# Causal attention in a decoder layer: every fourth head multiplies its weights by the values in fp32, the others in fp16 halves; one engine makes each low half, and ScalarE copies the keys

## The chip, the core and the metric

The kernel runs on one core of a Trainium2 chip. The core has five engines that run at the same time and wait for each other by semaphores: TensorE (PE in the rows; PEld is its weight load), VectorE (DVE), ScalarE (ACT), GpSimd (POOL) and SyncE (SP), which here starts the DMAs. The metric is the device time of one execution in microseconds (us).

## The reference

A decoder layer on x (4 x 512 x 512): attention, cross attention to a context, and a mixture of experts, each followed by a layer norm. Only the first part is touched by the change:

```python
q = (x @ Wq).reshape(B, S, 16, 32).transpose(0, 2, 1, 3)
c_kv = x @ Wkv_down
k = (c_kv @ Wk_up).reshape(B, S, 16, 32).transpose(0, 2, 1, 3)
v = (c_kv @ Wv_up).reshape(B, S, 16, 32).transpose(0, 2, 1, 3)
# 24 of the 32 columns of q and k are rotated (rope)
scores = jnp.where(causal, -jnp.inf, jnp.einsum('bhqd,bhkd->bhqk', qf, kf) * scale)
out = jnp.einsum('bhqk,bhkd->bhqd', softmax(scores), v)
```

## The kernel before

Fp32 numbers are multiplied on TensorE as two fp16 halves: a high half (the rounded number, a copy by ScalarE) and a low half (the number minus its high half, by VectorE or GpSimd). The attention runs over 4 batches of 512 tokens. In a batch there are 16 heads, each with 512 queries and keys in 4 blocks of 128. A loop body holds the heads of batch b and, woven between them, the projections of batch b+1; the first batch's projections stand ahead of the loop, and the last batch's heads behind it. What each engine does, and in which order, is written out by hand in the lists A_PE, A_ACT, A_DVE and A_POOL (L79 to L102), as steps "kind.number". An engine works its list strictly from left to right. Semaphores hold a step until what it needs is there.

The steps of one head i:

- `bq.i` (PE, L935): scores with queries on the partitions, into three PSUM banks; `max.i` (DVE, L1473): their row maxima, four reductions (nmf). The maxima of four heads are transposed (`mT`) and copied behind the queries (L1483), so that the second scores come out with the maximum taken off.
- `bk.i` (PE, L956): scores with keys on the partitions, 1280 columns for the causal triangle.
- `exp.i` (ACT, L1182): the exponential, PSUM to pf (fp32, 1280 columns, one of two buffers by i % 2).
- `hi.i` (ACT): phi, the fp16 copy of pf. `lo.i`: plo = pf - phi, columns 0 to 895 by POOL (L753) and 896 to 1279 by DVE (L1487). The next exp in the same buffer waits for both parts.
- `pv.i` (PE, L971): 10 pairs of blocks, each with phi and with plo as the weights and 65 columns of vcat moving: 32 high halves of the values, 32 low halves and a column of ones; 20 matmuls. `pv.i` (ACT): the 260 result columns to osb.
- `comb.j` (DVE, L1496 to L1498), for four heads at a time: reciprocal of the sums, adding the high and the low part, multiplying.

The projections of the next batch: `xT` (transposes of x), `c`, `row` (q rows and k rows by turns, ACT copies them to `rows`), `rope` (POOL, four operations), `rhi` and `rlo` (halves of the rows into cat: ACT L1144, DVE L1456), `v` (values: ACT high half, DVE low half, into vnext; SP moves vnext to vcat in two DMAs of 528 KB, L608), `cat0` and `cat1` (PE L923: eight transposes of cat into a PSUM bank, then one DVE copy of 96 x 1024 fp16 out of it, L1463, to qcT for even and kcT for odd numbers; cat0 holds heads 0 to 7, cat1 heads 8 to 15).

Ahead of the loop six expert weights get a low-rank product added (`fold`, L1540) and are stored back to DRAM (w_fold, L614); DVE's first step of the loop part waits for these stores.

Of the kernel before, what the change touches and what calls it, by code (L numbers as in the profile page):

```python
# [1880 lines left out]
```

## Time and profile before

| | us |
|---|---|
| time, median of 3 runs | 1698.6 (1692.5 to 1699.74) |
| the profiled execution | 1692.4, its span 1690.6 |
| VectorE busy in the span | 1273.0 (75%) |
| TensorE busy (modelled) | 1443.2 (85%) |
| ScalarE busy | 903.6 (53%) |
| GpSimd busy | 846.8 (50%) |

The span falls into a start (to 109 us), three turns of the attention loop (109 to 417 us, some 103 us each), the last batch's heads (to 485 us), the cross attention and the experts. The change touches only what lies before 485 us. Busy shares of the whole span say little of it; the stretches are read one by one below.

### The profile page before, as it was taken

What the parts mean: (1) busy time and instruction counts of PE and PEld (TensorE: products, weight loads), DVE (VectorE), ACT (ScalarE), POOL (GpSimd) and SP (SyncE); (2) the same over time, 40 slices, a digit from 0 to 9 for tenths busy, and PEclk for the clock granted to TensorE, in tenths of its full rate; (3) what the DMA queues carried; (4) which work ended last, traced back from release to release, by engine and by line L of the source; (5) the groups of instructions that cost most, each with busy time, mean ns of one, the idle gap of its engine ahead of it and who ended that gap; (6) DMA issues with size and microseconds to landing.
All of it is one profiled execution on the core that took longest, in us unless ns stands there. A gap on an engine that the chain in (4) does not pass through costs nothing.

```text
span 1690.6 us, 26867 instructions
## 1 busy us (share of the span) xinstructions
PE 1443.2 (85%) x9924; PEld 869.5 (51%) x9924; DVE 1273.0 (75%) x2115; ACT 903.6 (53%) x1431; POOL 846.8 (50%) x724
## 2 busy tenths in 40 slices
PE   4767787776668988848799999999999999999984
PEld 2345545444544444423356655666566655665553
DVE  4849899899867999975957767767766766766757
ACT  3327566565664544445455565556555565556542
POOL 6418385564352123687644654456454654466421
PEclk9969898989779999968999999999999999999997
DMA  9050010000211010110001000100101100100002
GB/s 282 26 200 2 28 51 2 28 26 27 100 51 50 26 70 32 51 63 13 25 26 38 26 26 29 35 26 26 37 26 31 33 26 26 38 26 26 13 1 100
DMA packets 63105, 74.62 MB, mean 44 GB/s; under 512 B 6912, under 2 KB 40320, under 8 KB 61952
## 3 DMA queue, kind: packets, MB, share of 16 engines
q1 hardware_dynamic: 62400, 68.68, 12.1%
q10 hardware_dynamic: 576, 4.19, 0.6%
q8 instruction: 84, 1.38, 0.3%
q14 instruction: 45, 0.37, 0.1%
HBM read 49.66 MB, written 10.49 MB: 36 GB/s over the span
## 4 chain that ended last, share of the span: by engine, by line
PE 60%; DVE 24%; issue 11%; ACT 3%; POOL 2%; DMA 1%; SPq 0%; DVEq 0%; POOLq 0%; ACTq 0%
PE banks L1103 48%; PE banks L870 6%; DVE nmf L1473 5%; DVE plo L1487 2%; PE banks L935 1%; DVE cat L1456 1%; PE banks L923 1%; DVE top L1599 1%; DVE wk L1595 1%; DVE att L1497 1%; DVE kcT L1463 1%; DMA w_fold<-w_top 1%; DVE attf L1606 1%; PE banks L1058 1%; DVE qcT L1483 1%
## 5 line engine op out<-in xcount | busy, mean ns | idle before, releaser
L1103 PE MATMUL banks<-xc,w 128*128 128x512 f16 x2688 | 591.2, 382 | 17.7 <-ACT banks L1144 15.0
L1103 PEld LDWEIGHTS banks<-xc,w 128*128 128x128 f16 x2688 | 264.2, 99 | 339.2 <-ACT banks L1144 20.2
L1103 PE MATMUL banks<-wd,mid 128*128 128x256 f16 x2688 | 298.1, 273 | 5.4 <-ACT banks L1144 3.1
L1103 PEld LDWEIGHTS banks<-wd,mid 128*128 128x128 f16 x2688 | 263.6, 98 | 40.9 <-ACT banks L1144 3.4
L847 POOL TENSOR_TENSOR mid<-m,mid 128x512 f16<-128x512 f32 x64 | 75.1, 1174 | 318.2 <-ACT mid L1144 318.2
L753 POOL TENSOR_TENSOR plo<-pf,phi 128x896 f16<-128x896 f32 x64 | 133.5, 2088 | 175.3 <-ACT phi L1144 175.2
L1144 ACT ACTIVATE banks<-banks 128x512 f32<-128x512 f32 x192 | 108.7, 579 | 193.0 <-PE banks L1103 193.0
L847 POOL TENSOR_TENSOR mid<-msum,mid 128x512 f16<-128x512 f32 x128 | 186.4, 1475 | 2.6 <-ACT mid L1144 2.6
L1421 DVE SCALAR_TENSOR_TENSOR w<-stage,w 128x512 f16<-128x512 f32 (+1 forms) x56 | 61.5, 1138 | 106.0 <-ACT w L1144 106.0
L1144 ACT ACTIVATE mid<-msum 128x512 f16<-128x512 f32 x128 | 81.2, 635 | 84.1 <-DVE msum L1780 28.1
L1473 DVE TENSOR_REDUCE nmf<-banks 128x1 f32<-128x512 f32 (+3 forms) x256 | 107.3, 480 | 14.9 <-PE banks L937 14.4
L1182 ACT ACTIVATE pf<-banks 128x1280 f32<-128x1280 f32 x64 | 79.2, 1238 | 40.5 <-PE banks L958 25.7
L935 PE MATMUL banks<-kcT,qcT 96*128 96x128 f16 (+3 forms) x256 | 66.0, 335 | 34.9 <-DVE nmf L1473 33.8
L1144 ACT ACTIVATE xc<-banks 128x512 f32<-128x512 f32 (+1 forms) x112 | 62.9, 599 | 49.1 <-PE banks L1058 26.7
L847 POOL TENSOR_TENSOR mid<-xc,mid 128x512 f16<-128x512 f32 x32 | 53.3, 1666 | 67.5 <-ACT mid L1144 67.5
L1144 ACT ACTIVATE phi<-pf 128x1280 f16<-128x1280 f32 x64 | 81.0, 1271 | 6.2 <-PE banks L971 6.0
L1742 DVE TENSOR_TENSOR xc<-banks,xc 128x512 f32<-128x512 f32 x96 | 63.3, 683 | 19.0 <-ACT banks L1144 19.0
L971 PE MATMUL banks<-vcat,phi 128*128 128x65 f16 x640 | 54.4, 205 | 26.7 <-DVE plo L1487 15.0
L1742 DVE TENSOR_TENSOR s<-banks,s 128x512 f32<-128x512 f32 x96 | 64.3, 685 | 15.0 <-PE banks L1103 15.0
L956 PE MATMUL banks<-qcT,kcT 100*128 100x512 f16 (+3 forms) x256 | 66.3, 336 | 9.6 <-ACT pf L1182 6.1
L1421 DVE SCALAR_TENSOR_TENSOR wd<-stage,wd 128x512 f16<-128x512 f32 (+1 forms) x32 | 28.3, 924 | 60.5 <-ACT wd L1144 60.5
L1144 ACT ACTIVATE s<-banks 128x512 f32<-128x512 f32 x96 | 56.3, 602 | 28.3 <-PE banks L1103 28.3
(252 smaller groups left out, 2910.8 us busy)
## 6 DMA issues: line engine op xcount, KB each, us to landing
stage<-w_fold SPq DMA_DIRECT2D x24, 256.0 KB, 3.0
stage<-in_Wg SPq DMA_DIRECT2D x24, 256.0 KB, 3.1
stage<-in_Wu SPq DMA_DIRECT2D x24, 256.0 KB, 3.1
stage<-in_Wd SPq DMA_DIRECT2D x24, 256.0 KB, 2.8
vcat<-vnext SPq DMA_DIRECT2D x8, 528.0 KB, 3.2
x_in<-in_x SPq DMA_DIRECT2D x4, 1024.0 KB, 6.3
x_res<-in_x SPq DMA_DIRECT2D x4, 1024.0 KB, 5.6
c_raw<-in_ctx SPq DMA_DIRECT2D x4, 1024.0 KB, 5.6
```

The costliest lines, as they stand in the source:

```text
L753: nc.gpsimd.tensor_tensor(plo[:, i % 2, 0:POOL_COLS], pf[:, i % 2, 0:POOL_COLS], phi[:, i % 2, 0:POOL_COLS], ALU.subtract).then_inc(p_lo_p ...
L847: nc.gpsimd.tensor_tensor(mid16[:, v % 3, 1, blk], mid_value(name), mid16[:, v % 3, 0, blk], ALU.subtract)\
L870: mm = nc.tensor.matmul(out, l(x, i), r(y, i), start=(i == 0 and j == 0), stop=(i == n - 1 and j == 2))
L935: nc.tensor.matmul(max_ps[:, o:o + w], qcT[0:K3, i, t * P:(t + 1) * P], kcT[0:K3, i, 0:w], start=True, stop=False)
L956: nc.tensor.matmul(st_ps[:, o:o + w], kcT[0:K3 + G, i, t * P:(t + 1) * P], qcT[0:K3 + G, i, t * P:S], start=True, stop=False)
L971: mm = nc.tensor.matmul(out, w[:, i % 2, o:o + P], vcat[:, i, t, 0:65], start=(t == 0 and x == 0), stop=(t == q and x == 1))
L1103: mm = nc.tensor.matmul(out, l(x, i), r(y, i), start=start and i == 0 and j == 0, stop=stop and i == k - 1 and j == 2, skip_group_check=True)
L1144: return nc.scalar.activation(out, in_, ACT.Copy, scale=scale)
L1182: nc.scalar.activation(pf[:, i % 2, :], st_ps[:, 0:TRI], ACT.Exp, scale=1.0 / (SQ * SQ * math.sqrt(HD))).then_inc(exp_done, 1)
L1421: return stt(out=out, in0=src, scalar=scale, in1=hi, op0=ALU.mult, op1=ALU.subtract)
L1473: nc.vector.tensor_reduce(nmf[:, t, i % G:i % G + 1], max_ps[:, o:o + w], AX, ALU.max, negate=True)\
L1742: tt_(saved, banks[:, k, :], saved, ALU.add).then_inc(c_sum, 1)
```

## The change

Each head is now one of two sorts. Heads 3, 7, 11 and 15 ("whole") have no halves: pv.i multiplies pf itself (fp32, as the weights) by 33 fp32 columns (32 values and the ones), 10 matmuls. Their steps hi.i and lo.i are gone, and the next exp in that buffer waits until TensorE has done pv.i. The other twelve ("halved") take 30 matmuls instead of 20: phi by the high halves and ones (33 columns), phi by the low halves (32 columns, added to the same result columns), plo by the high halves and ones (33); plo by the low halves is left out. A head's result is 33 columns wide, so the copy to osb moves 132 columns instead of 260, and comb has no adding step. The low half of a head is made whole (1280 columns) by one engine: DVE for heads 0, 4, 6, 8, 12, 14, POOL for 1, 2, 5, 9, 10, 13.

cat0 and cat1 are split in names: q0, q1 (even numbers; DVE copies them as before) and k0, k1 (odd numbers; now copied by ACT). The value weights are loaded in another order of heads, in four DMAs of 128-byte pieces, so that the whole heads' values lie together at the end; vnext and vcat hold fp32 or pairs of fp16 in the same bytes, 33 words a block; the move takes four pieces of 1056 bytes a partition instead of one of 4224. ACT writes the values in two copies (4 and 12 heads), DVE the low halves of 12 heads.

```diff
-    xT.0 xT.1 exp.0 xT.2 xT.3 exp.1 hi.0 hi.1 row.0 exp.2 c.0 pv.0 hi.2 row.1 rhi.0 exp.3 row.2 rhi.1 pv.1 hi.3
+    xT.0 xT.1 exp.0 k1.0 xT.2 xT.3 exp.1 hi.0 k1.1 hi.1 row.0 k1.2 exp.2 c.0 pv.0 hi.2 row.1 k1.3 rhi.0 exp.3 row.2 rhi.1 pv.1 
...
-    lo.14 maxn.3 v.3 lo.15 mTn.0 maxn.4 comb.3
+    lo.14 maxn.3 v.3 mTn.0 maxn.4 comb.3
...
-    lo.0 rope.0 lo.1 rope.1 lo.2 rope.2 rope.3 lo.3 rope.4 lo.4 rope.5 lo.5 rope.6 lo.6 rope.7 lo.7 lo.8 lo.9
-    lo.10 lo.11 lo.12 lo.13 lo.14 lo.15
+    rope.0 lo.1 rope.1 lo.2 rope.2 rope.3 rope.4 rope.5 lo.5 rope.6 rope.7 lo.9
+    lo.10 lo.13 
...
+LOW_DVE = (0, 4, 6, 8, 12, 14)
+LOW_POOL = (1, 2, 5, 9, 10, 13)
+HALVED = sorted(LOW_DVE + LOW_POOL)
...
+        vnext = sb(sa, "vnext", [P, H, TT, HD + 1])
+        vnext_halved = vnext[:, 0:H - G].rearrange("p h t n -> p (h t n)").bitcast(F16).rearrange("p (h t n) -> p h t n", h=H - G, t=TT)
+        vnext_whole = vnext[:, H - G:H]
...
+        def place(i):
+
+            return i % G * G + i // G
...
+        def wait_low(eng, b, i):
+
+            if i in LOW_DVE:
+                eng.wait_ge(p_lo_dve, b * len(LOW_DVE) + (LOW_DVE.index(i) + 1 + FREE))
+            elif i in LOW_POOL:
+                eng.wait_ge(p_lo_pool, b * len(LOW_POOL) + (LOW_POOL.index(i) + 1 + FREE))
...
-            sp.dma_start(raw_vu, a["Wvu"]).then_inc(w_loaded[3], 16)
+            for j in range(G):
+                sp.dma_start(raw_vu[:, j * P:(j + 1) * P].rearrange("p (g n) -> p g n", g=G),
+                             a["Wvu"].rearrange("p (g j n) -> j p g n", g=G, j=G)[j]).then_inc(w_loaded[3], 16)
...
-                heads = slice(half * 8, half * 8 + 8)
+                dst, src = (v[:, :, :, :].rearrange("p (j g) t n -> p j g (t n)", j=G)[:, :, 2 * half:2 * half + 2] for v in (vcat, vnext))
                 sp.wait_ge(a_ready["pv"], a_upto(b - 1, ("pv", half * 8 + 7)))
-                sp.dma_start(vcat[:, heads], vnext[:, heads]).then_inc(v_moved[half], 16)
+                sp.dma_start(dst, src).then_inc(v_moved[half], 16)
...
-                        pool.wait_ge(p_hi, b * H + (i + 1))
-                        nc.gpsimd.tensor_tensor(plo[:, i % 2, 0:POOL_COLS], pf[:, i % 2, 0:POOL_COLS],
-                                                phi[:, i % 2, 0:POOL_COLS], ALU.subtract).then_inc(p_lo_pool, 1)
+                        pool.wait_ge(p_hi, b * len(HALVED) + (HALVED.index(i) + 1))
+                        nc.gpsimd.tensor_tensor(plo[:, i % 2, :], pf[:, i % 2, :], phi[:, i % 2, :], ALU.subtract).then_inc(p_lo_pool, 1)
...
-                        pe.wait_ge(p_lo_pool, own * H + (i + 1 + FREE))
-                        pe.wait_ge(p_lo_dve, own * H + (i + 1 + FREE))
+                        wait_low(pe, own, i)
+                        if i not in HALVED:
+                            pe.wait_ge(exp_done, own * H + (i + 1 + FREE))
...
-                            out = bank[:, q * 65:(q + 1) * 65]
+                            out = bank[:, q * (HD + 1):(q + 1) * (HD + 1)]
                             for t in range(q + 1):
                                 o = OFF[TT - t] + (q - t) * P
-                                for x, w in enumerate((phi, plo)):
-                                    mm = nc.tensor.matmul(out, w[:, i % 2, o:o + P], vcat[:, i, t, 0:65],
-                                                          start=(t == 0 and x == 0), stop=(t == q and x == 1))
+                                if i not in HALVED:
+                                    mm = nc.tensor.matmul(out, pf[:, i % 2, o:o + P], vcat[:, place(i), t, :], start=t == 0, stop=t == q)
+                                    continue
+                                high, low = vcat_halved[:, place(i), t, 0:HD + 1], vcat_halved[:, place(i), t, HD + 2:2 * HD + 2]
+                                nc.tensor.matmul(out, phi[:, i % 2, o:o + P], high, start=t == 0, stop=False)
+                                nc.tensor.matmul(out[:, 0:HD], phi[:, i % 2, o:o + P], low, start=False, stop=False)
+                                mm = nc.tensor.matmul(out, plo[:, i % 2, o:o + P], high, start=False, stop=t == q)
...
-                        scaled(vnext[:, :, i, 0:HD], a_bank(u).rearrange("p (h n) -> p h n", h=H), SV / (SX * SW))\
-                            .then_inc(a_hi[k], 1)
+                        src = a_bank(u).rearrange("p (h n) -> p h n", h=H)
+                        scaled(vnext_whole[:, :, i, 0:HD], src[:, H - G:H], SV / (SX * SW)).then_inc(v_whole, 1)
+                        scaled(vnext_halved[:, :, i, 0:HD], src[:, 0:H - G], SV / (SX * SW)).then_inc(a_hi[k], 1)
+                    elif k in ("k0", "k1"):
+                        act.wait_ge(a_ready[k], a_upto(own, u))
+                        half = int(k[1])
+                        if i == 0:
+                            act.wait_ge(st_ready, (own - 1) * H + (8 * half + 8 + FREE))
+                        scaled(kcT[0:K3, half * 8:half * 8 + 8, i * P:(i + 1) * P],
+                               a_bank(u).bitcast(F16)[0:K3, :].rearrange("p (h n) -> p h n", h=8), 1.0).then_inc(a_drained[k], 1)
...
-                        act.wait_ge(p_lo_pool, g + (FREE - 1))
-                        act.wait_ge(p_lo_dve, g + (FREE - 1))
+                        of, before = (own, i - 2) if i >= 2 else (own - 1, i + H - 2)
+                        if before in HALVED:
+                            wait_low(act, of, before)
+                        else:
+                            act.wait_ge(a_ready["pv"], a_upto(of, ("pv", before)))
...
-                        nc.vector.tensor_copy((qcT, kcT)[i % 2][0:K3, half * 8:half * 8 + 8, i // 2 * P:(i // 2 + 1) * P],
+                        nc.vector.tensor_copy(qcT[0:K3, half * 8:half * 8 + 8, i * P:(i + 1) * P],
...
-                        dve.wait_ge(p_hi, own * H + (i + 1))
-                        tt_(plo[:, i % 2, POOL_COLS:TRI], pf[:, i % 2, POOL_COLS:TRI], phi[:, i % 2, POOL_COLS:TRI],
-                            ALU.subtract).then_inc(p_lo_dve, 1)
+                        dve.wait_ge(p_hi, own * len(HALVED) + (HALVED.index(i) + 1))
+                        tt_(plo[:, i % 2, :], pf[:, i % 2, :], phi[:, i % 2, :], ALU.subtract).then_inc(p_lo_dve, 1)
...
-                        chain.link(nc.vector.reciprocal(rsum[:, :, :], src[:, :, :, 64]))
-                        chain.link(tt_(o4, src[:, :, :, 0:HD], src[:, :, :, HD:2 * HD], ALU.add))
-                        tt_(o4, o4, rsum[:, :, :].unsqueeze(3).to_broadcast([P, G, TT, HD]), ALU.mult).then_inc(comb_done, 1)
+                        chain.link(nc.vector.reciprocal(rsum[:, :, :], src[:, :, :, HD]))
+                        tt_(o4, src[:, :, :, 0:HD], rsum[:, :, :].unsqueeze(3).to_broadcast([P, G, TT, HD]), ALU.mult).then_inc(comb_done, 1)
```

What stands in a row on VectorE before, from the copy of head rows (kcT, step cat0.5) to the copy of the maxima (L1483), late in the loop body; cat is rlo.7, the two plo are lo.9 and lo.10:

```order
L1463 COPY kcT<-banks 96x8x128
L1454 REGISTER_ALU
L1456 TENSOR_TENSOR cat<-rows,cat 128x16x32
L1487 TENSOR_TENSOR plo<-pf,phi 128x384
L1459 REGISTER_ALU
L1463 COPY qcT<-banks 96x8x128
L1459 REGISTER_ALU
L1463 COPY kcT<-banks 96x8x128
L1487 TENSOR_TENSOR plo<-pf,phi 128x384
L1480 REGISTER_ALU
L1483 COPY qcT<-banks 4x2048
```

And at the same place now; the plo is lo.8, the two cat are rlo.6 and rlo.7:

```order
L1531 TENSOR_TENSOR plo<-pf,phi 128x1280
L1498 REGISTER_ALU
L1500 TENSOR_TENSOR cat<-rows,cat 128x16x32
L1498 REGISTER_ALU
L1500 TENSOR_TENSOR cat<-rows,cat 128x16x32
L1503 REGISTER_ALU
L1507 COPY qcT<-banks 96x8x128
L1527 COPY qcT<-banks 4x2048
```

The two 384-column pieces and the two key copies are gone from here; one 1280-column piece stands ahead, and what is left is two cat, one query copy and the copy of the maxima.

ScalarE at the same stretch before: pf is exp, phi hi, osb the copy of pv's result, cat rhi.7.

```order
L1144 ACTIVATE phi<-pf 128x1280
L1182 ACTIVATE pf<-banks 128x1280
L1144 ACTIVATE osb<-banks 128x260
L1144 ACTIVATE phi<-pf 128x1280
L1144 ACTIVATE cat<-rows 128x16x2x32
L1182 ACTIVATE pf<-banks 128x1280
L1144 ACTIVATE osb<-banks 128x260
L1144 ACTIVATE phi<-pf 128x1280
```

ScalarE now, from exp.8 to k0.2:

```order
L1225 ACTIVATE pf<-banks 128x1280
L1176 ACTIVATE osb<-banks 128x132
L1176 ACTIVATE kcT<-banks 96x8x128
L1176 ACTIVATE phi<-pf 128x1280
L1176 ACTIVATE cat<-rows 128x16x2x32
L1225 ACTIVATE pf<-banks 128x1280
L1176 ACTIVATE osb<-banks 128x132
L1176 ACTIVATE kcT<-banks 96x8x128
```

Two key copies (kcT, k0.1 and k0.2) stand between the exponentials, and one of the two phi is gone (head 7 is whole).

TensorE at head 3, from the third block of values' projection on, before (the first of twenty):

```order
L889 REGISTER_ALU
L870 MATMUL banks<-wvu,cT 128x512 x3
L971 MATMUL banks<-vcat,phi 128x65
L971 MATMUL banks<-vcat,plo 128x65
L971 MATMUL banks<-vcat,phi 128x65
L971 MATMUL banks<-vcat,plo 128x65
```

and now (the ISA row is a wait; what follows is the scores of head 11):

```order
L913 REGISTER_ALU
L894 MATMUL banks<-wvu,cT 128x512 x3
L999 MATMUL banks<-vcat,pf 128x33 x10
L952 ISA
L962 MATMUL banks<-kcT,qcT 128x128
```

Ten fp32 matmuls of 33 columns stand where twenty fp16 ones of 65 stood.

## Rows read from the trace of the kernel before

**Rows 1.** The stretches (start:end us, then their length and the busy us of each engine).
```profile
core 0: us, PE busy (x) PEld busy (x) DVE busy (x) ACT busy (x) POOL busy (x), PEclk, DMA share, GB/s
...
109.20:211.40 102.20, 79.99 (x877) 57.15 (x878) 87.08 (x145) 64.11 (x78) 59.10 (x49) 0.90 0.09 33
211.40:314.30 102.90, 76.61 (x821) 51.86 (x820) 93.55 (x154) 63.44 (x78) 60.39 (x49) 0.90 0.09 33
314.30:417.00 102.70, 75.38 (x829) 50.22 (x826) 96.49 (x159) 63.32 (x75) 64.57 (x50) 0.92 0.06 22
417.00:485.00 68.00, 43.16 (x530) 33.03 (x531) 57.49 (x91) 42.65 (x52) 30.33 (x14) 0.77 0.22 78
```

**Rows 2.** The chain by line over 211.4:314.3 (the answer cuts the line).
```profile
by line: issue 25.0%; DVE nmf L1473 17.4%; PE banks L870 8.2%; DVE plo L1487 7.3%; PE banks L935 5.3%; PE banks L923 3.4%; DVE kcT L1463 3.2%; DVE att L1497 2.8%; PE banks L956 2.6%; DVE qcT L1483 2.5%; DVE resid L1518 2.2%; PE banks L937 2
```

**Rows 3.** VectorE groups in 211.4:314.3 (line, op, xcount | busy, mean ns | idle).
```profile
L1487 DVE TENSOR_TENSOR plo<-pf,phi 128x384 f16<-128x384 f32 x16 | 17.0, 1060 | 0.0
...
L1463 DVE COPY kcT<-banks 96x1024 f16<-96x1024 f16 x8 | 5.4, 679 | 0.6 <-PE banks L923 0.6
...
L1497 DVE TENSOR_TENSOR att<-osb 128x512 f32<-128x512 f32 x4 | 4.2, 1049 | 0.1
...
L1421 DVE SCALAR_TENSOR_TENSOR vnext<-banks,vnext 128x512 f16<-128x512 f32 x4 | 2.7, 680 | 0.0
```

**Rows 4.** What TensorE waited for in 211.4:314.3 (total us, times, longest).
```profile
PE banks L935 <- DVE nmf L1473: 6.6, 4, 3.9
...
PE banks L971 <- DVE kcT L1463: 3.0, 1, 3.0
```

**Rows 5.** The low halves over the whole run (ns min/median/max).
```profile
L753 POOL TENSOR_TENSOR plo<-pf,phi x64: 1875/1996/3673, 117.9 to 479.1; 128x896 f16<-128x896 f32 x64
L1487 DVE TENSOR_TENSOR plo<-pf,phi x64: 527/681/2272, 117.9 to 479.4; 128x384 f16<-128x384 f32 x64
```

**Rows 6.** Order in time, 265.2 to 270 us (start, duration).
```profile
265.27 2.26 POOL L753 TENSOR_TENSOR plo<-pf,phi 128x896 f16<-128x896 f32 x1 [1.99 <-ACT phi L1144]
265.83 2.12 DVE L1487 TENSOR_TENSOR plo<-pf,phi 128x384 f16<-128x384 f32 x1
```

**Rows 7.** ScalarE groups in 211.4:314.3.
```profile
L1144 ACT ACTIVATE phi<-pf 128x1280 f16<-128x1280 f32 x17 | 21.5, 1270 | 1.9 <-PE banks L971 1.9
...
L1144 ACT ACTIVATE cat<-rows 128x1024 f16<-128x1024 f32 x8 | 8.4, 1055 | 0.3 <-POOL rows L748 0.3
L1144 ACT ACTIVATE osb<-banks 128x260 f32<-128x260 f32 x16 | 6.2, 384 | 7.4 <-PE banks L971 7.4
```

**Rows 8.** TensorE, one head of the values product, 218.35 us on.
```profile
218.35 0.19 PE L971 MATMUL banks<-vcat,phi 128*128 128x65 f16 x1
...
218.94 0.19 PE L971 MATMUL banks<-vcat,plo 128*128 128x65 f16 x1
```

**Rows 9.** TensorE, a small fp16 product over the whole run.
```profile
L1089 PE MATMUL banks<-wr,xc 128*128 128x16 f16 x128 | 3.6, 174 | 1.6 <-DVE xc L1421 1.6
```

**Rows 10.** Fp32 transposes: their four weight loads in one burst (start, us).
```profile
509.25 0.42 PEld L1058 LDWEIGHTS banks<-identf,x1row 128*128 128x128 f32 x4 [2.31 <-DVE woT L1421]
```

**Rows 11.** Eight fp32 transposes in the first loop turn (start, duration of the eight).
```profile
111.94 1.97 PE L895 MATMUL banks<-identf,x_in 128*128 128x128 f32 x8
```

**Rows 12.** VectorE groups in the last batch, 417:485.
```profile
L1487 DVE TENSOR_TENSOR plo<-pf,phi 128x384 f16<-128x384 f32 x15 | 15.8, 1061 | 4.5 <-ACT phi L1144 4.4
...
L1497 DVE TENSOR_TENSOR att<-osb 128x512 f32<-128x512 f32 x4 | 5.6, 1394 | 0.1
```

**Rows 13.** The chain by line in the last batch.
```profile
by line: DVE nmf L1473 18.4%; issue 15.2%; DVE plo L1487 14.9%; DVE att L1497 7.2%; PE banks L971 4.8%; PE banks L935 4.0%; ACT phi L1144 3.8%; DVE qcT L1483 3.6%; DVE wqw L1421 3.2%; DVE stats L1509 3.1%; DVE resid L1506 2.7%; DVE att L149
```

**Rows 14.** VectorE groups at the start, 68:90.
```profile
L1463 DVE COPY kcT<-banks 96x1024 f16<-96x1024 f16 x4 | 2.7, 684 | 0.9 <-PE banks L923 0.7
```

**Rows 15.** The chain near 16 us: the low half of another weight (start, us).
```profile
16.18 7.97 DVE wq L1421
```

**Rows 16.** The chain in order of time, 88 to 110 us (start, us).
```profile
96.97 12.19 DMA w_fold<-w_top
```

More of the change, by code:

```diff
@@ L110 @@
     fold.0 fold.1 row.0 c.0 row.1 rhi.0 row.2 rhi.1 row.3 v.0 fold.2 rhi.2 row.4 rhi.3 v.1 fold.3 v.2 row.5 rhi.4 fold.4
[L111 removed]
+    row.6 rhi.5 fold.5 row.7 rhi.6 rhi.7 k0.0 k0.1 k0.2 k0.3 v.3
 """)
@@ L311, in decoder @@
         plo = sb(sa, "plo", [P, 2, TRI], F16)
-        osb = sb(sa, "osb", [P, 2, G, TT, 65])
+        osb = sb(sa, "osb", [P, 2, G, TT, HD + 1])
+        raw_small = sb(sa, "raw_small", [P, 1024])
         nmf = sb(sa, "nmf", [P, TT, G])
@@ L437, in decoder @@
         x2_kept = sem("x2_kept")
-        la_loaded = [sem(f"la{n}_loaded") for n in range(6)]
-        lb_loaded = [sem(f"lb{n}_loaded") for n in range(6)]
+        factors_loaded = [sem(f"factors{n}_loaded") for n in range(6)]
         wf_loaded = [sem(f"wf{n}_loaded") for n in range(6)]
@@ L917, in heads @@
                         three(bank, lambda x, j: cT[:, x, i * P:(i + 1) * P], lambda y, j: wvu[:, y, :], 1, done)
-                    elif k in ("cat0", "cat1"):
-                        pe.wait_ge(cat_lo, own * (2 * TT) + (i + 1 + FREE))
+                    elif k in ("q0", "k0", "q1", "k1"):
+                        row = 2 * i + (k[0] == "k")
+                        pe.wait_ge(cat_lo, own * (2 * TT) + (row + 1 + FREE))
                         out = bank.bitcast(F16)
                         for j in range(8):
-                            src = cat[:, i, (k == "cat1") * 8 + j].rearrange("p a n -> p (a n)")
+                            src = cat[:, row, (k[1] == "1") * 8 + j].rearrange("p a n -> p (a n)")
                             mm = nc.tensor.transpose(out[0:K3, j * P:(j + 1) * P], src, ident16[:, :])
@@ L999, in _ @@
                     heads(next_part(A_PE, A_NEXT), None, 0, [], at, at + 1)
-            at = next_part(A_PE, A_NEXT).index(("cat0", 0))
+            at = next_part(A_PE, A_NEXT).index(("q0", 0))
             pe.wait_ge(lora_added, 24)
             heads(next_part(A_PE, A_NEXT), None, 0, [], at)
-            for k in ("xT", "c", "row", "v", "cat0"):
+            for k in ("xT", "c", "row", "v", "q0", "k0"):
                 pe.wait_ge(a_drained[k], a_upto(0, (k, A_PER[k] - 1)))
@@ L1012, in _ @@
             pe.wait_ge(exp_done, B * H + FREE)
-            for k in ("cat1", "mT", "pv"):
+            for k in ("q1", "k1", "mT", "pv"):
                 pe.wait_ge(a_drained[k], a_upto(B - 1, (k, A_PER[k] - 1)))
@@ L1191, in heads @@
                             act.wait_ge(comb_done, own * (H // G) + (i // G - 1 + FREE))
-                        scaled(osb[:, i // G % 2, i % G], a_bank(u)[:, 0:TT * 65].rearrange("p (t n) -> p t n", t=TT), 1.0)\
+                        scaled(osb[:, i // G % 2, i % G], a_bank(u)[:, 0:TT * (HD + 1)].rearrange("p (t n) -> p t n", t=TT), 1.0)\
                             .then_inc(a_drained[k], 1)
@@ L1224, in _ @@
             last = own_part(A_ACT, A_NEXT)
-            at = last.index(("hi", 13))
+            at = last.index(("hi", 14))
             heads(last[:at], B - 1, None)
```

93 lines of the change are left out of this document (49 added, 44 removed).

## The prediction

> **What bounds the kernel now.** I read the stretches first [rows 1]. The change touches only what lies before 485 us: three loop turns of 102.2, 102.9 and 102.7 us and the last batch of 68.0. In the turn 211.4:314.3 VectorE is busy 93.6 us of 102.9, in the next one 96.5; TensorE shows 76.6 (with the modelled ends of its matmuls in it), ScalarE 63.4, GpSimd 60.4. So VectorE is full and the others have room. The chain of that turn [rows 2] agrees: nmf, plo, kcT, att and qcT lie on it, plo with 7.3%, kcT with 3.2%, att L1497 with 2.8%; much of its "issue" lies between such steps. And TensorE waits for VectorE: 6.6 us for the maxima, 3.0 us in one piece for a key copy that still held the PSUM bank of pv [rows 4]. In the last batch VectorE is busy 57.5 of 68.0 [rows 1], plo has 14.9% of the chain and att L1497 7.2% [rows 13].
>
> VectorE's pieces are longer than their work. The 384-column plo takes 527 ns at best and 1060 in the mean [rows 3, 5]. One case is laid open [rows 6]: GpSimd starts its plo at 265.27 and ends at 267.53; VectorE starts at 265.83 and takes 2.12 us instead of 0.53, so it ends 0.42 us after GpSimd. One stands still until the other is through. The Trainium skill (SBUF — State Buffer, "SBUF: two separate sides") says that a VectorE operation with two SBUF inputs and a GpSimd operation share a port pair as an exclusive lock, held for the whole instruction. The trace agrees with its 2.12 us. By that rule a longer GpSimd instruction blocks longer, which speaks against whole 1280-column pieces on GpSimd.
>
> **The change, for one loop turn.**
>
> Low halves on VectorE: 16 pieces go, 17.0 us [rows 3]. Six of 1280 columns come. In proportion to the best case one is 0.527 x 1280/384 = 1.76 us alone (a little much, since the fixed part is scaled too). Blocked behind a whole GpSimd piece it would be 1.76 + 2.85 = 4.6, where 2.85 is 1996 ns x 1280/896 [rows 5]. Today's mean block is 1060 - 527 = 0.53 us; GpSimd loses 16 x 2.0 = 32 us of plo and gets 6 x 2.85 = 17, so it is there a quarter less, in longer pieces. I take a block of 0.35, so 2.1 us each, near the lower end because the trace's mean block is far below a whole piece. 6 x 2.1 = 12.6: -4.4 us (bounds -6.4 and +10.6).
>
> Key copies: 8 x 679 ns leave VectorE: -5.4 us [rows 3].
>
> comb: the adding step goes, 4 x 1049 ns: -4.2 us [rows 3]. The multiplication reads osb in place of att; same size, no price.
>
> Low halves of values: 12 of 16 heads, 384 columns for 512, a quarter of the 4 x 680 ns: -0.6 us [rows 3], at most.
>
> VectorE in all: -14.6 us of 93.6. That is the gain if every microsecond of VectorE is one of the turn. By the chain it is less: plo 7.3% of 102.9 is 7.5 us and falls by 4.4/17.0, so 1.9; kcT 3.3; att 2.9: -8.1 us. I take the middle, -11.4.
>
> TensorE. Halved heads: 30 matmuls of 33 columns for 20 of 65. Twenty take 0.62 us today, 31 ns apart [rows 8]; the nearest small product, 16 columns, comes every 3.6/128 = 28 ns [rows 9]. 30 x 0.028 = 0.84, +0.22 each, x12 = +2.6 us. Whole heads: no fp32 product stands in this trace, only fp32 transposes. Four weight loads of these take 0.42 us, 0.105 each [rows 10]; eight transposes in the first turn took 1.97, 0.246 each [rows 11]. Bounds 0.028 (as fp16) and 0.246. I take two loads' worth, 0.21 us, near the dear end, since the weights are fp32 as in those rows and a product has more to do than a transpose: 10 x 0.21 = 2.1 against 0.62, +1.5, x4 = +5.9. Together +8.5 us (bounds +1.3 and +9.9), and TensorE has 26 us idle in the turn, most of them waits for VectorE that shrink. On the chain TensorE's lines have some 21% [rows 2], so I count 21% of 8.5: +1.8.
>
> The Trainium skill (FP8 and Floating Point Precision, "TensorE Precision Notes") says that true fp32 takes four passes through the array. By it a product could be four of the 0.105 us steps instead of the two that I took, and the sum per turn would be about 7 us poorer; that is the first rival below.
>
> ScalarE. The eight key copies have 1024 columns; the cat copy of that width takes 1055 ns: +8.4. Four phi go, 4 x 1270: -5.1. osb falls from 260 to 132 columns, at most half of 16 x 384 ns, I take -1.7. The second values copy adds four starts, at most 4 x 0.2. In all +2.4 on 63.4 [rows 7]: hidden in 39 us of idle time. What stands behind a key copy (exp.9 behind k0.1, say) is late by up to 1.06 us; heads 7 and 11 lack their phi just there. Of the waits: exp after a whole head in its buffer waits for TensorE's pv, and that stands in TensorE's list behind scores that wait for the maxima. Before, it waited for plo, which stood behind the same maxima in VectorE's list. No price, but a rival.
>
> GpSimd: 60.4 - 15 = 45 us, never last.
>
> A turn: -11.4 + 1.8 = -9.6; three of them: -28.8 us.
>
> **Last batch.** plo 15.8 to 12.6: -3.2; add -5.6 [rows 12]: -8.8 at most. By the chain 10.1 us x 3.2/15.8 = 2.1, and 4.9: -7.0. Middle -7.9. TensorE's +8.5 is dearer at the mean clock of 0.77 there [rows 1], some +10, and pv and scores have 9% of the chain [rows 13]: +0.9. -7.0 us.
>
> **Start.** Four key copies, 2.7 us, leave VectorE [rows 14]; each copy also waits for its transposes, so half: -1.4. The value weights arrive in 128-byte pieces; VectorE wants them only behind the 7.97 us of another weight's low half [rows 15], so no price. The values' move in pieces of a quarter stands in SP's queue ahead of the five stores whose landing ends the stretch, 12.19 us of DMA [rows 16]: +0.4, a guess inside 0 and 2. -1.0 us. In later turns that move ends long before pv.0 asks for it.
>
> **Sum.** -28.8 - 7.0 - 1.0 = -36.8. The profiled execution took 1692.4 (span 1690.6), so 1655.6, say 1656. It is the lowest of the runs shown (median 1698.6), so the median after may lie up to 6 us higher. Under 0.5%, 8.5 us, a measurement can't tell a change from none; faster means below 1690.1.
>
> **Rivals.**
>
> A, TensorE becomes the bound: an fp32 product works as four of the 0.105 us steps. A whole head is 4.2 us, +3.6, x4 = 14.3, with the halved ones 16.9: TensorE busy 93.5 of 102.9, and what is left is little more than its unavoidable waits. A turn gains 2, the last batch 2, the start 1: 1692.4 - 9 = 1683. For it: no row shows the product, and the page's four passes. Against: 26 us of idle time, and a queue of 33-column work, not of 128.
>
> B, slower: ScalarE becomes the place where TensorE's banks hang. Each key copy comes up behind an exp or a phi (1.27) and is 0.38 longer than VectorE's: 8 x 1.65 = 13.2 us; each of the four exps behind a whole head waits out the longest wait for maxima, 3.9 us [rows 4]: 15.6. Of these 28.8 us more than 9.6 must reach the chain before a turn gets longer. With half, 14.4, a turn is 4.8 longer: 1692.4 + 14.4 = 1707. Against: ScalarE is a third idle, and VectorE's own key copies stand behind maxima today.
>
> C, all of VectorE's time comes through: plo at 1.76 each, another -2.0, so -16.6 a turn, x3 = 49.8; last batch -10.8; start -2.7: 1629. For it: a share busy of 91 to 94%.
>
> **Chances.** Forecast 0.56, C 0.17, A 0.17, B 0.10. Faster: 0.53 + 0.17 + 0.10 = 0.80. Same: 0.02 of the forecast, 0.05 of A, 0.02 of B: 0.09. Slower: 0.01 + 0.02 + 0.08 = 0.11. The range goes from C to a little above the time before, 1628 to 1694; the forecast's own is 1642 to 1672.
>
> **What the profile after would show.** The first maxima of successive turns some 93 us apart instead of 103. VectorE busy about 79 us a turn, its 1280-column plo 2.1 us in the mean; near 3 means that the block by GpSimd grew. The ten fp32 matmuls of a whole head 2.1 us: 1 us means C, over 4 us A, with TensorE's queue the releaser of nmf. Waits of pv and of the scores for the key copies on ScalarE (kcT) above 10 us a turn mean B. The stretch from 485 us on must be unchanged; a difference there is nothing of this argument. The forecast is wrong if the turns shrink by less than 5 or more than 14 us.

## The result

1688.2 us, median of ten executions (1685.9 to 1693.9), against 1698.2 of the kernel before, ten on the same chip. The ratio is 0.9945, 95% interval 0.9926 to 0.9964: faster by about half a percent, 10 us, where 42 below the median were forecast (37 below the profiled execution). The profiled execution after took 1688.9, its span is 1687.0; from profile to profile 3.6 us are left of the span. Two later executions of the kernel before, of 3489 and 5135 us, are slow ones and stand in no ratio.

The stretches of the kernel after, cut at the same events as [rows 1] (start:end us, length, busy us of PE, PEld, DVE, ACT and POOL, granted clock, DMA share, GB/s):

```profile
117.10:217.80 100.70, 86.94 (x997) 65.00 (x998) 68.26 (x122) 65.73 (x86) 43.32 (x38) 0.90 0.10 34
217.80:313.80 96.00, 80.03 (x941) 57.53 (x940) 76.29 (x132) 64.57 (x86) 42.97 (x38) 0.93 0.11 35
313.80:409.90 96.10, 80.93 (x948) 58.30 (x946) 77.69 (x134) 64.97 (x85) 44.10 (x39) 0.91 0.07 24
409.90:483.70 73.80, 58.16 (x656) 47.70 (x657) 43.02 (x79) 40.38 (x53) 14.65 (x6) 0.64 0.21 72
483.70:1687.00 1203.30, 1105.53 (x6538) 643.49 (x6536) 876.27 (x1480) 637.42 (x1104) 587.64 (x512) 0.96 0.11 34
```

VectorE's busy time fell by more than forecast: 17.3 us in the second turn. That turn became 6.9 us shorter, the first one 1.5, the third 6.6. The last batch became longer (it ends here at a GpSimd step whose twin before starts at 486.4; 417.0:486.4 is 69.4 us, so +4.4), and the first turn begins 7.9 us later. The rest is 0.9 shorter, which is taken as no effect of the change. So 15.0 were won in the turns and 12.3 lost at the two ends.

The groups of the second turn that answer to [rows 3, 5, 7] (line, engine, op, shapes, xcount | busy us, mean ns | idle before it and its releasers):

```profile
L778 POOL TENSOR_TENSOR plo<-pf,phi 128x1280 f16<-128x1280 f32 x6 | 15.7, 2614 | 18.1 <-ACT phi L1176 17.9
...
L1531 DVE TENSOR_TENSOR plo<-pf,phi 128x1280 f16<-128x1280 f32 x6 | 9.0, 1508 | 0.9 <-ACT phi L1176 0.9
...
L1176 ACT ACTIVATE kcT<-banks 96x1024 f16<-96x1024 f16 x8 | 8.1, 1017 | 3.3 <-PE banks L948 3.3
...
L1507 DVE COPY qcT<-banks 96x1024 f16<-96x1024 f16 x8 | 5.5, 687 | 6.9 <-PE banks L948 6.9
...
L1176 ACT ACTIVATE osb<-banks 128x132 f32<-128x132 f32 x16 | 4.4, 277 | 4.8 <-PE banks L999 4.2 <-PE banks L1004 0.5
```

VectorE now has time to wait: 6.9 us for the transposes before the q copies. And a whole head's product, L999, appears as a releaser of ScalarE. The next rows show it in the second turn (40 products; the last two lines are who waited for it, in us, and how often), then in the last batch (PE group by shape), then the chain of the turn 217.8:313.8, and then that of the last batch, 409.9:483.7:

```profile
L999 PEld LDWEIGHTS banks<-vcat,pf x80: 190/192/192, 242.3 to 301.4; 128*128 128x128 f32 x80
L999 PE MATMUL banks<-vcat,pf x80: 193/277/278, 242.5 to 301.4; 128*128 128x33 f32 x80
...
  ACT osb L1176: 4.2, 1
  ACT pf L1225: 3.5, 2
```

```profile
L999 PE MATMUL banks<-vcat,pf 128*128 128x33 f32 x80 | 15.7, 370 | 0.4 <-ACT osb L1176 0.4
```

```profile
by line: issue 15.2%; PE banks L894 10.7%; DVE nmf L1517 10.6%; PE banks L983 7.1%; PE banks L999 6.9%; PE banks L948 6.2%; PE banks L962 5.9%; ACT pf L1225 4.6%; ACT cat L1176 3.2%; DVE resid L1560 3.1%; PE banks L985 2.8%; ACT kcT L1176 2
```

```profile
by line: PE banks L999 20.5%; PE banks L983 10.2%; DVE nmf L1517 9.8%; issue 8.1%; PE banks L962 7.3%; ACT pf L1225 6.8%; DVE qcT L1527 5.0%; PE banks L985 3.6%; DVE wqw L1464 3.1%; PE banks L964 2.7%; ACT wqw L1176 2.4%; DVE resid L1560 2.
...
425.77 4.22 PE banks L999 x20
446.20 2.22 PE banks L999 x20
460.36 4.23 PE banks L999 x20
...
476.13 4.49 PE banks L999 x20
```

In the last batch the products of the four whole heads, 15.2 us, lie whole on the chain: 20.5%, where pv had 4.8% [rows 13]. The ten products of one head take 2.22 us at full clock and 4.22 to 4.49 at or near the 1.2 GHz level; three of the four heads fell into the slower one. In the turn the chain has L999 with 6.9% of 96.0 us, 6.6 us of the 8.9 that four heads take.

### The profile page after: what moved, and what is told of

Its sections match the earlier page's. It is cut to its first block, busy times and chain, and to the rows that moved or that the text cites. A ratio compares the mean times of both kernels' runs of the same rounds, so it can differ in the third digit from the quotient of the medians.

```text
span 1687.0 us, 27697 instructions
## 1 busy us (share of the span) xinstructions
PE 1480.7 (88%) x10404; PEld 907.4 (54%) x10404; DVE 1199.2 (71%) x2027; ACT 908.2 (54%) x1463; POOL 777.4 (46%) x685
## 3 DMA queue, kind: packets, MB, share of 16 engines
q1 hardware_dynamic: 67440, 68.68, 12.6%
## 4 chain that ended last, share of the span: by engine, by line
PE 66%; DVE 15%; issue 10%; ACT 5%; POOL 2%; SPq 1%; DMA 1%; DVEq 0%; ACTq 0%; POOLq 0%
PE banks L1135 48%; PE banks L894 7%; DVE nmf L1517 2%; PE banks L999 2%; PE banks L948 2%; PE banks L962 2%; PE banks L983 2%; ACT pf L1225 1%; DVE top L1641 1%; DVE wk L1637 1%; DVE attf L1648 1%; DMA w_fold<-w_top 1%; PE banks L964 1%; PE banks L985 1%; PE banks L1090 1%
## 5 line engine op out<-in xcount | busy, mean ns | idle before, releaser
L871 POOL TENSOR_TENSOR mid<-m,mid 128x512 f16<-128x512 f32 x64 | 75.1, 1173 | 319.7 <-ACT mid L1176 319.7
L778 POOL TENSOR_TENSOR plo<-pf,phi 128x1280 f16<-128x1280 f32 x24 | 63.2, 2641 | 119.3 <-ACT phi L1176 118.9
L768 POOL TENSOR_TENSOR turn_a<-rows,cossin 128x384 f32<-128x384 f32 x32 | 34.8, 1088 | 153.1 <-ACT rows L1176 152.3
L948 PE MATMUL banks<-ident,cat 128*96 128x128 f16 x512 | 45.4, 244 | 25.0 <-DVE xT L1464 13.4
```

Source lines behind the costliest of these rows:

```text
L778: nc.gpsimd.tensor_tensor(plo[:, i % 2, :], pf[:, i % 2, :], phi[:, i % 2, :], ALU.subtract).then_inc(p_lo_pool, 1)
L871: nc.gpsimd.tensor_tensor(mid16[:, v % 3, 1, blk], mid_value(name), mid16[:, v % 3, 0, blk], ALU.subtract)\
L948: mm = nc.tensor.transpose(out[0:K3, j * P:(j + 1) * P], src, ident16[:, :])
```

## The experiments

Sixteen runs, in three groups: the whole heads' product, the other parts of the change, and the start. One table holds the same three numbers of each trace, in us: when the first turn begins (VectorE's first xT low half of the loop); how long the three turns take, from there to the first adding of x_res (resid<-att,x_res, L1506 before, L1548 after) that follows the third turn; and the last batch, from there to the next first adding. "Time" is the median, "ratio" that to executions of the kernel before on the same chip, whose medians were 1698.4 to 1698.8. In e2, e6 and e11 the result is no longer that of the reference: they leave out the fp32 product and keep its order and its waits. In the code cuts "..." stands for what is left out.

| | first turn at | turns | last batch | time | ratio (95%) |
|---|---|---|---|---|---|
| before | 109.3 | 302.7 | 73.5 | 1698.4 | |
| after | 117.0 | 288.1 | 76.9 | 1688.2 | 0.9945 (0.9926-0.9964) |
| e1 Wvu in one DMA | 117.4 | 285.4 | 75.6 | 1687.4 | 0.9923 (0.9899-0.9948) |
| e2 one pass | 117.2 | 271.3 | 65.4 | 1661.1 | 0.9767 (0.9741-0.9794) |
| e3 own buffer | 113.9 | 276.8 | 75.1 | 1674.4 | 0.9848 (0.9819-0.9877) |
| e4 keys on VectorE | 116.5 | 282.1 | 81.0 | 1686.2 | 0.9916 (0.9890-0.9942) |
| e5 all halved | 111.4 | 285.1 | 66.0 | 1671.0 | 0.9851 (0.9823-0.9880) |
| e6 e2 and e3 | 117.0 | 271.3 | 65.5 | 1660.8 | 0.9782 (0.9750-0.9813) |
| e7 low halves shared | 115.5 | 287.2 | 79.6 | 1691.9 | 0.9955 (0.9935-0.9976) |
| e8 e3 and e4 | 116.3 | 281.5 | 74.2 | 1685.0 | 0.9923 (0.9897-0.9949) |
| e9 after again | 117.3 | 285.2 | 76.9 | 1686.3 | one execution |
| e10 before again | 109.4 | 306.2 | 73.6 | 1694.6 | one execution |
| e11 e2 in last batch | 115.5 | 289.9 | 65.1 | 1674.2 | 0.9851 (0.9822-0.9880) |
| e12 e5, tail dealt anew | 119.1 | 283.8 | 65.9 | 1673.4 | 0.9831 (0.9805-0.9857) |
| e13 before, 0.9 us later | 113.8 | 305.1 | 71.2 | 1699.5 | 1.0002 (0.9980-1.0025) |
| e14 before, 0.45 us later | 117.9 | 303.8 | 73.5 | 1699.4 | 1.0005 (0.9986-1.0023) |
| e15 after, earlier | 111.0 | 286.5 | 77.0 | 1689.9 | 0.9957 (0.9933-0.9980) |
| e16 e5, earlier | 118.5 | 285.3 | 65.1 | 1675.3 | 0.9852 (0.9825-0.9880) |

Equal and nearly equal kernels show how exact one trace is: before, e10, e13 and e14 have 302.7 to 306.2 in the turns, after and e9 288.1 and 285.2. The last batch repeats within 2.4 us. A difference of 3 us or less in the turns or in the last batch is therefore none.

### The whole heads' product

e2. The four whole heads read the upper 16 bits of the same words.

```diff
-mm = nc.tensor.matmul(out, pf[:, i % 2, o:o + P], vcat[:, place(i), t, :], ...)
+half = lambda x: x.bitcast(F16).rearrange("p (n two) -> p n two", two=2)[:, :, 1]
+mm = nc.tensor.matmul(out, half(pf[:, i % 2, o:o + P]), half(vcat[:, place(i), t, :]), ...)
```

> The changed kernel, but the whole heads' ten products read the upper 16 bits of pf and of the values as fp16 (every second half-word), so each is one pass instead of two; all waits, copies and buffers are the same; what the products compute is different. Theory 'fp32 time': the loss against the forecast is TensorE's time for 16 x 10 fp32 products (2.22 us a head at the full clock, 4.23 at the half one, against 0.3 or so). Then a turn falls from 96.0 by 4 us or more and the last batch from 73.8 by 8 or more: 20 us or more in all, ratio 0.982 or lower. Rival 'hold': what costs is that exp two heads later waits for pv's place in TensorE's list, whatever its length; then a turn falls by under 2 us and the time by under 8.

27 us less than the changed kernel. Ten products take 0.41 us at full clock. The turns become 16.8 us shorter (13.9 against e9), the last batch 11.5. Both parts then stand about where the forecast had them for VectorE's savings alone: 31.4 us less than before in three turns (forecast 3 x 11.4), 8.1 less in the last batch (7.9). What is not separated is the clock: the granted one in the last batch is 0.78 before, 0.67 after, 0.70 in e2 and 0.74 in e11, so a part of the 11.5 may be other work at a higher clock.

e11. The same in the last batch only.

```diff
+half = lambda x: x.bitcast(F16)...[:, :, 1] if isinstance(own, int) else x
```

> The changed kernel, and only in the last batch the four whole heads read the upper fp16 halves in one pass (left out: the fp32 product of those four heads). One pass in all batches gave -27 us, of which its trace had 11.5 in the last batch, where the clock is half and each fp32 product takes 4.2 us. If the last batch pays by itself: 1688 - 11.5 = 1677, the turns as in the changed kernel. If what it gave there came from earlier work that the turns had made ready: within 4 us of 1688.

14 us less; the last batch is 65.1 us, as in e2 (-11.8), and the turns are as they were (289.9). The last batch pays by itself.

e3. The whole heads' exp writes to a buffer of its own (pfw, which is raw_small enlarged to 1280), and pv reads it there. It waits for the whole head four back, long done; and the halved head two behind a whole one, which used to wait for that head's product, now waits for the low half of the head four back.

```diff
+back = 4 if i not in HALVED or (i - 2) % H not in HALVED else 2
...
-nc.scalar.activation(pf[:, i % 2, :], st_ps[:, 0:TRI], ...)
+nc.scalar.activation(pf[:, i % 2, :] if i in HALVED else pfw[:, :], st_ps[:, 0:TRI], ...)
```

> The changed kernel, but whole heads write their exponential to a third buffer of their own; an exp then waits for a head four back instead of for TensorE's pv of the head two back. Theory 'hold': the added wait of exp for pv, 18.2 us in 8 pieces in the profile, is what ate the gain; then a turn falls by 3 to 4 us, the last batch by 3 or more, and the ratio is 0.986 or lower. Rival 'fp32 time': TensorE does the same work in the same order, so the waits only change their name: under 4 us in all, ratio 0.992 to 0.996.

14 us less. The trace has 11.3 less in the turns (8.4 against e9), 1.8 in the last batch, which is none, and 3.1 that belong to the start (below); what follows the last batch is 2.3 longer. In the turns the hold of the buffer matters; in the last batch it is the product itself.

e6. Both.

> Both at once: whole heads read the upper fp16 halves in one pass (left out: the fp32 product itself) and their exp has a buffer of its own. The one-pass run gave -27 us and the own buffer -14. If the two are the same cost (exp waits because the product is long and late), together they give little over the one-pass run: 1655 to 1661. If they are separate (TensorE's time, and a wait through TensorE's list), they add: 1647. Taken: 1657.

As e2 alone: turns 271.3 in both. With a short product an own buffer brings nothing. So the hold is no second cost, but one way in which a long product reaches ScalarE; e3 gave back about two thirds of what e2 did in the turns.

e5. All sixteen heads in halves: low halves of 3 and 11 on VectorE, of 7 and 15 on GpSimd; osb of 132 columns, one engine for each low half and key copies on ScalarE stay.

```diff
-LOW_DVE = (0, 4, 6, 8, 12, 14)
-LOW_POOL = (1, 2, 5, 9, 10, 13)
+LOW_DVE = (0, 3, 4, 6, 8, 11, 12, 14)
+LOW_POOL = (1, 2, 5, 7, 9, 10, 13, 15)
```

> All sixteen heads are multiplied in fp16 halves, 3 and 11 with their low half on VectorE, 7 and 15 on GpSimd; osb of 132 columns, low halves by one engine and key copies by ScalarE stay. Per turn VectorE gets 2 x 1.5 = 3.0 us, ScalarE 4 x 1.27 = 5.1, GpSimd 2 x 2.6, and TensorE loses 4 x (2.22 - 0.84) = 5.5. If the whole heads are what eats the gain (fp32 product and the exp that waits for it), this is faster than the changed kernel by much of what the one-pass run gave: 1665 to 1678 us. If VectorE still sets the turn, it is slower: 3.0 x 3 + 3 = 12 us more, 1700. Taken: 1672.

17 us less than the changed kernel, though VectorE, ScalarE and GpSimd all have more to do (VectorE 83.3 us in the second turn against 76.3). Where it comes from matters: 10.9 us are won in the last batch and 5.6 at the start, but the turns, 285.1, are those of the changed kernel within what equal kernels differ (288.1 and 285.2). In the turns a whole head is thus worth about as much as a halved one; it seems that what it spares the other engines it costs on TensorE. In the last batch it only costs. The chain there (396.5:462.5) is led by VectorE and ScalarE again:

```profile
by line: DVE nmf L1512 17.8%; issue 13.9%; ACT pf L1221 10.3%; PE banks L959 7.1%; ACT phi L1173 7.0%; POOL plo L775 4.0%; DVE qcT L1522 3.7%; DVE plo L1526 3.7%; DVE stats L1546 3.2%; PE banks L980 3.0%; DVE resid L1543 2.9%; PE banks L961
```

e12. e5 with the last low halves dealt anew.

```diff
-LOW_DVE = (0, 3, 4, 6, 8, 11, 12, 14)
+LOW_DVE = (0, 3, 4, 6, 8, 11, 13, 15)
```

> All sixteen heads in halves (as in the run that gave 1671), and the last low halves dealt anew: 13 and 15 on VectorE (1.5 us each), 12 and 14 on GpSimd (2.6), since GpSimd's low half of head 15 was the last but one step on the chain. If single low halves still count: 1 to 3 us less, 1669. If the chain only moves to head 14: 1671 to 1673.

No gain: last batch 65.9, and the chain only moves to GpSimd's low half of head 14, 3.56 us of it.

### The other parts of the change

e7. The twelve low halves shared again.

```diff
-nc.gpsimd.tensor_tensor(plo[:, i % 2, :], pf[:, i % 2, :], phi[:, i % 2, :], ALU.subtract)...
+nc.gpsimd.tensor_tensor(plo[:, i % 2, 0:POOL_COLS], pf[:, i % 2, 0:POOL_COLS], phi[:, i % 2, 0:POOL_COLS], ALU.subtract)...
...
-tt_(plo[:, i % 2, :], pf[:, i % 2, :], phi[:, i % 2, :], ALU.subtract)...
+tt_(plo[:, i % 2, POOL_COLS:TRI], pf[:, i % 2, POOL_COLS:TRI], phi[:, i % 2, POOL_COLS:TRI], ALU.subtract)...
```

> Each low half is again shared, 896 columns on GpSimd and 384 on VectorE, for the twelve halved heads; all else as changed. VectorE's six pieces of 1.5 us (9.1 a turn) become twelve of about 0.9 (10.8), GpSimd's six of 2.64 become twelve of 2.0. If giving each half to one engine brought its share, this is slower than the changed kernel: VectorE +1.7 us a turn, 6 to 8 us in all, 1695. If what counts is how long a single low half takes from phi to product (GpSimd alone 2.64 us against 2.0 shared, and the halves on GpSimd lie on the last batch's chain), it is faster: twelve halves in the last batch, six of them 0.6 shorter, 2 to 4 us, and about as much in the turns, 1682. Taken: 1692.

The same as the changed kernel. POOL_COLS is 896. VectorE's busy time hardly moves (76.0 in the second turn): the twelve shared pieces take 10.4 us there, six whole ones 9.0. Giving each half to one engine brought nothing that can be measured.

e4. k0 and k1 by VectorE in its old places (one line of the order shown). e8: the same with e3's buffer.

```diff
-    xT.0 xT.1 q1.0 max.5 xT.2 xT.3 q1.1 res.0 lo.0 q1.2 max.6 res.1 c.0 q1.3
+    xT.0 xT.1 q1.0 k1.0 max.5 xT.2 xT.3 q1.1 res.0 k1.1 lo.0 q1.2 max.6 k1.2 res.1 c.0 q1.3
```

> The changed kernel, but all key copies are back on VectorE, each behind the query copy as before. If VectorE's time is still what bounds a turn, this gives back 5.4 us a turn, some 16 us, ratio 1.004. If TensorE and its waits bound it now (VectorE is busy 76 of 96 us), it costs under 2 us a turn, and the start and the copies that TensorE waited for on ScalarE gain 2 to 4 us: ratio 0.992 to 0.998.

> Own buffer for the whole heads' exp, and the key copies back on VectorE (0.68 us each there, 1.03 on ScalarE). Alone these gave -14 and -2 us. If ScalarE is what the banks wait for once the hold is gone, they add or more: 1668 to 1672. If VectorE is now what ends the turn, the copies' 5.4 us a turn come back: 1680. Taken: 1673.

e4 alone makes no difference that can be measured (the intervals overlap; 6.0 less in the turns, 3.1 against e9, and 4.1 more in the last batch). With the own buffer (e8 against e3) the medians stand 11 us apart, 1685.0 where 1673 was taken, so what e8 took was wrong. The traces have 4.7 of it in the turns and 2.4 at the start; the rest is not placed. As long as the product holds things up VectorE has room for the copies; once the hold is gone, a part of their 5.4 us a turn comes back.

e1. One DMA for Wvu; the halves of it are made in four copies each, which put the heads in order.

```diff
-for j in range(G):
-    sp.dma_start(raw_vu[:, j * P:(j + 1) * P]..., a["Wvu"]...[j]).then_inc(w_loaded[3], 16)
+sp.dma_start(raw_vu, a["Wvu"]).then_inc(w_loaded[3], 16)
```

> The changed kernel, but the value weights come in one DMA again, in the order of DRAM; ScalarE and VectorE put the heads in order when they make the halves (four copies of 128 columns each). Theory 'start': the loop begins 7.9 us later than before because four DMAs of 128-byte pieces hold SyncE's queue for 5.67 us instead of 0.49 and all loads behind them come late. Then the loop should begin at 110 to 112 us instead of 117.1, and the time be 5 to 7 us below the changed kernel's (ratio to before 0.990 to 0.992). Rival: the delay comes from the key copies on ScalarE and the clock between 70 and 97 us; then the loop begins at 114 us or later and the ratio stays at 0.994.

No difference that can be measured, and the first turn begins at 117.4, where the changed kernel had 117.0: the 128-byte pieces are not what makes the start late.

### The start

The first turn begins 7.9 us later in the profile of the changed kernel, and TensorE's granted clock in 68:80 differs. That stretch in before, after, e13, e14 and e15, in this order (columns as above):

```profile
68.00:80.00 12.00, 5.69 (x72) 4.45 (x72) 8.89 (x16) 0.59 (x1) 0.00 (x0) 1.00 0.00 1
```

```profile
68.00:80.00 12.00, 8.76 (x58) 6.00 (x56) 6.71 (x11) 3.96 (x4) 1.86 (x3) 0.55 0.01 2
```

```profile
68.00:80.00 12.00, 6.67 (x66) 4.15 (x64) 10.23 (x18) 2.71 (x3) 3.79 (x6) 1.00 0.01 3
```

```profile
68.00:80.00 12.00, 7.97 (x55) 5.10 (x53) 9.37 (x16) 2.71 (x3) 4.22 (x6) 0.77 0.00 1
```

```profile
68.00:80.00 12.00, 5.79 (x72) 4.41 (x72) 5.79 (x10) 4.65 (x5) 0.00 (x0) 0.93 0.00 1
```

With 0.93 to 1.00 here the first turn begins at 109 to 114, with 0.54 to 0.77 at 115 to 119, in all eighteen traces. (0.5 is the 1.2 GHz level, 1.00 the 2.4.) TensorE's work just ahead does not tell the two apart: between 55 and 65 us it is busy 10.0 of 10 us in after, but in e3 and e13 too, which have the full clock in 68:80; in before it is 8.8.

e9 and e10. Both kernels once more.

> The changed kernel once more, for its start. In its first profile TensorE's granted clock was 0.55 from 68 to 80 us and 0.50 from 80 to 100, and the first turn began at 117.0; before the change 1.00, 0.62 and 109.3. If the clock there follows from the kernel, this shows again under 0.65 from 68 to 80 us and a start of the turn at 115 to 118. If it is chance from execution to execution, it may show 1.00 and 109 to 114.

> The kernel before the change once more, for its start. If the clock there follows from the kernel: again 1.00 from 68 to 80 us and a start of the first turn at 109 to 110. If chance: it may show under 0.65 and 112 to 117.

Both showed the same as the first time. That looked like a property of the kernel. The changed one begins its work 0.3 us later (GpSimd's memsets, 5.06 against 4.75 us) and its product behind cT 0.8 later. So four kernels move the moment alone:

```diff
 pool.memset(nm16[:, :, :], 0.0).then_inc(consts, 1)
+pool.memset(phi[:, 0, 0:1024], 0.0).then_inc(consts, 1)
```

> The kernel before the change with one more memset of 1024 fp16 columns on GpSimd ahead of TensorE's first work: everything begins some 0.9 us later. If lateness alone decides what clock is granted at the start: a dip at 46 to 50 us, a clock under 0.65 from 68 to 80, first turn at 115 to 118 in place of 109.3, and 6 to 8 us more in all, 1705. If the changed work itself does it: 1.00 from 68 to 80, first turn at 110.2, 1699.

> The same with 512 columns, 0.45 us later. TensorE's product behind cT should begin at 33.7 to 33.9 us, between the traces at 33.6 (first turn at 111.4) and 33.9 (113.9). If lateness decides: first turn at 111 to 114 and 1700 to 1703. If not: 109.8 and 1699.

> The changed kernel with the memset of nm16 (0.52 us) moved from GpSimd to VectorE, so that TensorE's first work begins some 0.4 us earlier, as before the change. If the moment decides: full clock from 68 to 80 us, first turn at 110 to 114, and 3 to 7 us less, 1683. If the changed work decides: clock 0.55 to 0.6, first turn at 116.6, 1688.

> All sixteen heads in halves, and the same memset moved. Its sister at 1671 had its first turn at 111.4 us, the one with the last low halves dealt anew at 119.1. If the moment decides and 0.4 us earlier is still within full clock: first turn at 110 to 111, 1668 to 1671. If chance decides: anywhere from 1668 to 1678.

The diff is e13's; e14 has 512 columns, e15 and e16 have nm16's memset on VectorE. The moment of the product behind cT did not follow the edits in proportion (33.3 us before, 34.5 in e13, 35.0 in e14), so they move it, but not by a set amount. In the traces the kernel before, held back, begins its first turn at 113.8 and 117.9, so it can lose the 8 us too; the changed one, earlier, begins at 111.0; but e16, e5 made earlier, begins at 118.5 where e5 had 111.4. And the medians of e13 and e14 are those of the kernel before, and e15's is that of the changed kernel: seven of its nine executions took 1687 to 1691, two 1681, and the profile is of one of those two. The kernel before ranges from 1689 to 1706. So the moment alone does not decide.

What the record suggests is that the start is early in some executions and late in others of one kernel. No kernel was profiled with both, but every execution has its mean granted clock. e15's two short executions have 0.931, its other seven 0.921 to 0.925. Both profiles of the kernel before have 0.936, which 4 of its 62 executions beside e1 to e16 reach; 41 of them have 0.929 or less, like e14, whose late start is in its trace with 0.927. How often each kernel has which start is not shown. If most executions of the kernel before start late, the two profiles of it are lucky ones, and the fair pair of traces is e14 and after: first turn at 117.9 and 117.0, times 1699.0 and 1688.9. That is 10.1 us, the difference of the medians.

## Why the prediction was wrong

The sign was right; the size by the medians was a quarter of what was forecast (10 us against 42). In the profiled executions 33 us are missing (forecast -36.8, measured -3.5). By stretch: the turns won 15.0 where 28.8 were forecast, 13.8 missing; the last batch became 4.4 longer where 7.0 were to be won, 11.4 missing; the start came 7.9 later instead of 1.0 earlier, 8.9 missing; the rest gave 0.9.

- **"On the chain TensorE's lines have some 21% [rows 2], so I count 21% of 8.5: +1.8."** This step failed. The product was sized well: 2.22 us for ten against 2.1, at full clock. But 7.2 us a turn of product time (4 x (2.22 - 0.41)) gave back 16.8 over three turns when e2 took it away: 77% of 21.7 (64% by the repeat of the changed kernel), not 21%. The chain of the second turn says the same: 6.6 of 8.9 us of the products lie on it, and TensorE's lines have some 40% of it where they had 21%. A share of the chain says how much of the old path is TensorE's. New work that stands between an exp and the next one is on the new path for the most part.
- **"TensorE's +8.5 is dearer at the mean clock of 0.77 there [rows 1], some +10, and pv and scores have 9% of the chain [rows 13]: +0.9."** The same step in the last batch, and here it is the largest term. Three of the four heads' products run at or near the lower level: 15.2 us in all, whole on the chain. Taking them away gives 11.5 (e2) and 11.8 (e11) back, at a somewhat higher clock. Without them the last batch is 8.1 to 8.4 shorter than before, where -7.9 was forecast for VectorE.
- **"No price, but a rival"**: exp waits for TensorE's pv behind a whole head. It had a price, 8 to 11 us over the turns (e3), but only through the long product (e6). The waits for the key copies that were rival B's sign stayed small, about 1 us in the second turn.
- **Rival A** had the wrong size and nearly the right time (1683). It asked for 4.2 us a whole head; 2.22 was enough to make TensorE what holds the turn up most.
- **VectorE: -14.6 us a turn.** Right and a little low: -17.3. The low halves went from 17.0 us to 9.0, not to 12.6. Of these 8.0 us 6.6 came with twelve heads in place of sixteen (e7 has 10.4) and 1.4 with the single engine. The 1280-column plo took 1.51 us, not 2.1. In the trace none of VectorE's 24 whole pieces runs at the same time as one of GpSimd's, so the block that "speaks against whole 1280-column pieces on GpSimd" was not put to the test. Of VectorE's saving a turn would have had -10.5 (e2), near the -11.4 taken. That the middle of two sums came so close is luck as far as the runs show: none takes VectorE's saving alone.
- **Low halves by one engine and key copies** brought no time that can be measured (e7, e4), the copies not until the hold is gone (e8). With all heads in halves the whole change is worth 17.6 us in the turns and 7.5 in the last batch (e5). How it divides between the narrower osb, the adding step and the rest was not tried.
- **Start, -1.0.** Measured +7.9 in the profiles, but at a lower granted clock in 68:80, which kernels that differ by one memset show or do not. It is no term of the change as far as the medians tell; its cause stays open. With a late start on both sides the change is worth 10.1 us, and 27 of the 37 forecast are missing. e2 gave 27 back, of which 6.3 stood in the forecast (3 x 1.8 and 0.9) as TensorE's price; so the product accounts for some 21 of the 27, and the other 6 are spread over small terms that no run takes apart.

## What to carry to other kernels

When work moves from a full engine to another, don't weigh the new work by that engine's share of the old chain: ask between which two steps of the next chain it stands, and count it whole if nothing runs beside it. Price it once more at the clock of each stretch; here the same ten products took 2.2 us at full clock and 4.2 to 4.5 for three of the four heads of the last batch. Then compare with the plain alternative, stretch by stretch: here the product broke even with the halves in the turns and lost 11 us in the last batch. And a difference between two single profiles at the start of a kernel needs a second profile of both, and the medians, before it is given to the change.

## What the runs showed of the hardware

- An fp32 product with 33 columns moving has two matmul records and two weight-load records and takes 0.222 us at full clock; each weight load shows 190 to 192 ns. The same product read as fp16 takes 0.041.
- GpSimd's subtraction (fp32 and fp16 in, fp16 out) takes 2.61 us for 1280 columns, 2.04 ns each; VectorE's 1.51, 1.18 ns each.
- A PSUM copy of 132 fp32 columns on ScalarE takes 277 ns; of 1024 fp16 columns on 96 partitions 1017 ns, where VectorE takes 687.
- The mean granted clock of one and the same stretch, 68:80, was 0.93 to 1.00 in some traces and 0.54 to 0.77 in others, of kernels that differ by as little as one memset; the first turn then begins at 109.3 to 113.9 or at 115.5 to 119.1.
